# A second buffer for each stage of the pieces of G, in an attention and feed-forward layer on one Trainium2 core

## The reference

```
queries = (query @ Wq + bq); keys_flat = key_param @ Wk + bk
values = keys_flat @ Wv + bv
A = sparsemax(einsum('blhe,bshe->bhls', queries, keys) / sqrt(E))
out = einsum('bhls,bshd->blhd', A, values)   # transposed to (B, H, L, D), then
out = transpose(out, (0, 2, 1, 3)).reshape(B, L, H * D) @ Wo + bo
x = layernorm(x + out)
s = x @ Win + bin_; h = relu(s[..., None] * W1 + b1)
g = einsum('btmh,mh->btm', h, W2) + b2
x = layernorm(x + g @ Wout + bout)
```

## Time and profile before

| | |
|---|---|
| median of three runs | 1370.93 us |
| the profiled execution | 1371.21 us, span 1369.4 us |
| PE busy | 1238.4 us (90%) |
| DVE busy | 1155.0 us (84%) |
| ACT busy | 1078.6 us (79%) |
| POOL busy | 851.5 us (62%) |
| mean granted TensorE clock | 0.952 |
| HBM read, written | 273.24 MB, 58.72 MB |

### The profile page before, as it was taken

How to read it: one execution, slowest core, us unless ns; L and a number is a source line. 1 busy time by engine, 2 the same in 40 slices (tenths; PEclk the granted TensorE clock), 3 DMA queues, 4 the chain that set the end, 5 groups by cost and what they waited for, 6 DMA issues and landing times. The chain is left out here.

```text
span 1369.4 us, 25981 instructions
## 1 busy us (share of the span) xinstructions
PE 1238.4 (90%) x6104; PEld 917.0 (67%) x6104; DVE 1155.0 (84%) x4538; ACT 1078.6 (79%) x2317; POOL 851.5 (62%) x1676
## 2 busy tenths in 40 slices
PE   9954557599999999999999999999999999989885
PEld 6632334477777777777777777777777777756552
DVE  4847555798999999999999999999999999957666
ACT  3634254467899999999999999999999999977666
POOL 1532334454567777777777777777777767766654
PEclk9976667899999999999999999999999999999998
DMA  6455355898778788888888888888888888789983
GB/s 202 124 135 146 76 143 147 235 333 254 247 259 268 266 265 263 270 274 270 266 266 266 261 270 273 276 263 268 266 263 265 271 275 265 241 268 345 333 274 100
DMA packets 96793, 333.89 MB, mean 244 GB/s; under 512 B 16580, under 2 KB 16580, under 8 KB 80231
## 3 DMA queue, kind: packets, MB, share of 16 engines
q1 hardware_dynamic: 96470, 331.76, 76.4%
q10 hardware_dynamic: 144, 0.26, 0.1%
HBM read 273.24 MB, written 58.72 MB: 242 GB/s over the span
## 5 line engine op out<-in xcount | busy, mean ns | idle before, releaser
L825 PE MATMUL bank<-G_sb,pT 128*128 128x512 f32 x512 | 244.5, 600 | 11.1 <-DMA G_sb<-G_of_heads 9.9
L1462 DVE MAX8 top<-bank 128x8 f32<-128x32 f32 x2048 | 211.4, 175 | 0.0
L816 PE MATMUL bank<-A_hi,xT_hi 128*128 128x512 f32 x512 | 205.3, 401 | 0.0
L817 PE MATMUL bank<-A_lo,xT_hi 128*128 128x512 f32 x512 | 205.2, 401 | 0.0
L818 PE MATMUL bank<-A_hi,xT_lo 128*128 128x512 f32 x512 | 204.7, 400 | 0.0
L1512 DVE SCALAR_TENSOR_TENSOR acc<-hinge,w2c,acc 128x512 f32<-128x512 f32 x210 | 156.5, 745 | 51.9 <-ACT hinge L1096 51.7
L605 POOL TENSOR_TENSOR rstd<-ve,minus_half 128x1 f32<-128x1 f32 x244 | 172.9, 709 | 43.0 <-POOL ve L600 42.7
L1066 ACT ACTIVATE unread<-y_sb,minus_mean 128x512 bf16<-128x512 f32 x244 | 174.5, 715 | 24.6 <-POOL minus_mean L592 23.6
L1096 ACT ACTIVATE hinge<-s_sb,b1c,w1c 128x512 f32<-128x512 f32 x240 | 192.6, 805 | 0.0
L592 POOL TENSOR_TENSOR minus_mean<-sum,per_row 128x1 f32<-128x1 f32 x244 | 86.1, 359 | 133.9 <-DVE y_sb L1355 133.6
L1355 DVE SCALAR_TENSOR_TENSOR y_sb<-bank,y_sb 128x512 f32<-128x512 f32 x244 | 159.3, 657 | 10.0 <-DMA y_sb<-in_L_attn_query_dram 8.8
(11 more groups left out here) (172 smaller groups left out, 3144.8 us busy)
## 6 DMA issues: line engine op xcount, KB each, us to landing
G_sb<-G_of_heads SPq DMA_DIRECT2D x128, 1536.0 KB, 7.7
x_sb<-in_L_attn_query_dram SPq DMA_DIRECT2D x128, 256.0 KB, 6.5
y_sb<-in_L_attn_query_dram SPq DMA_DIRECT2D x256, 128.0 KB, 7.2
out_dram<-o_sb SPq DMA_DIRECT2D x230, 128.0 KB, 6.5
G_of_heads<-y_sb SPq DMA_DIRECT2D x96, 256.0 KB, 4.1
out_dram<-y_sb SPq DMA_DIRECT2D x11, 256.0 KB, 3.3
y_sb<-in_L_attn_Wk_dram SPq DMA_DIRECT2D x1, 1024.0 KB, 5.7
y_sb<-in_L_attn_Wq_dram SPq DMA_DIRECT2D x1, 1024.0 KB, 7.9
```

The costliest lines, as they stand in the source:

```text
L816: nc.tensor.matmul(ps[:], hi[:, c, :], w_hi[:, c, :], start=start and c == 0, stop=False)
L817: nc.tensor.matmul(ps[:], hi[:, c, :], w_lo[:, c, :], start=False, stop=False)
L825: nc.tensor.matmul(o[:], p_blocks[:, block_of(i, c), i % HPC, :], G[:, raw_col(c), :].bitcast(F32), start=(c == RAW[0]), stop=False)
L1462: mx = nc.vector.max(top8[:, h, :], z_ps[i % 2][:, h * S:(h + 1) * S])
```

## The change

Each of the three stages gets a second buffer, used in turns by successive units of its kind:

- plain: rows 0 to 3 of `y_sb`, and the four rows of `o_sb` (the ring of the finished rows, not used before slot 36);
- rests: rows 4 to 7 and 8 to 11 of `y_sb`;
- rounded parts: four of the six rows in `G_sb` buffer 1, and in buffer 2.

ScalarE waits, before it fills a buffer, for the stores of the unit before the last one of its kind. SyncE stores plain and rounded parts in its slot u+6 instead of u+7; rests stay in slot u+8. The loads of G for heads 1 and 2, which overwrite the rounded parts' buffers, wait for their stores and for the subtractions that read them. The waits ahead of the y loads follow the new rows. The row of b_out, loaded at the start and read at slot 25, moves from `o_sb` to `both`. ScalarE's and POOL's instructions stay in the order in which they were, with other tiles; the rest is now written as plain float32, without rounding.

```diff
-        STAGE_RAW, STAGE_LO, STAGE_HI = 0, HPC, 2 * HPC
+        def stage_raw(k):
+            return (y_sb[:, 0:HPC, :], o_sb[:])[k // (2 * HPC) % 2]
+        def stage_lo(k):
+            first = HPC * (1 + k // (2 * HPC) % 2)
+            return y_sb[:, first:first + HPC, :]
+        def stage_hi(k):
+            return G_sb[:, 1 + k // (2 * HPC) % 2, 0:HPC, :]
...
@@ SyncE, slot
-                for k in pieces(turn, j - 2)[HPC - 1:]:
+                for k in pieces(turn, j - 1)[HPC - 1:]:
                     heads, c, a = piece(k)
                     if in_parts(k):
                         sp.wait_ge(s_Ghi, parts_to(k))
-                        store_unit(heads, hi_col(c), STAGE_HI, s_Gst_hi)
+                        store_unit(heads, hi_col(c), stage_hi(k).bitcast(F32), s_Gst_hi)
                     else:
                         sp.wait_ge(s_Gev, k + 1)
-                        store_unit(heads, raw_col(c), STAGE_RAW, s_Gst_raw)
+                        store_unit(heads, raw_col(c), stage_raw(k), s_Gst_raw)
                 for k in pieces(turn, j - 3)[HPC - 1:]:
                     heads, c, a = piece(k)
                     if in_parts(k):
                         sp.wait_ge(s_Glo, parts_to(k))
-                        store_unit(heads, lo_col(c), STAGE_LO, s_Gst_lo)
+                        store_unit(heads, lo_col(c), stage_lo(k), s_Gst_lo)
...
+                    if i in (1, 2):
+                        sp.wait_ge(s_Glo, PIECES // 2 - (HPC if i == 1 else 0))
+                        sp.wait_ge(s_Gst_hi, 16 * (PIECES // 2 - (HPC if i == 1 else 0)))
...
-                    for row, s_stored in ((STAGE_RAW, s_Gst_raw), (STAGE_LO, s_Gst_lo), (STAGE_HI, s_Gst_hi)):
-                        if base + i == row:
-                            sp.wait_ge(s_stored, 16 * (PIECES // 2))
+                    if base + i == 0:
+                        sp.wait_ge(s_Gst_raw, 16 * (PIECES // 2))
+                    if base + i == HPC:
+                        sp.wait_ge(s_Gst_lo, 16 * (PIECES // 2))
@@ POOL, slot
-                        nc.gpsimd.tensor_tensor(y_sb[:, STAGE_LO + a, :].bitcast(F32R), y_sb[:, STAGE_LO + a, :],
-                                                y_sb[:, STAGE_HI + a, :], ALU.subtract).then_inc(s_Glo, 1)
+                        lo, hi = stage_lo(k)[:, a, :], stage_hi(k)[:, a, :]
+                        nc.gpsimd.tensor_tensor(lo, lo, hi.bitcast(F32), ALU.subtract).then_inc(s_Glo, 1)
@@ ScalarE, slot
-                    stored = 16 * HPC * (k // HPC // 2)
+                    stored = 16 * HPC * (k // HPC // 2 - 1)
                     if in_parts(k):
-                        if a == 0 and k >= 2 * HPC:
+                        if a == 0 and stored > 0:
                             act.wait_ge(s_Gst_hi, stored)
                             act.wait_ge(s_Gst_lo, stored)
```

More of the change, by code:

```diff
@@ L193, in build_kernel @@
         Wout_sb = s_sb[:, 0, :]
-        bout_row = o_sb[0:1, 2, :]
+        bout_row = both[0:1, :]
         rounded = split[0:1, :]
@@ L487, in store_unit @@
                     sp.dma_start(places[:, :, col * D:(col + 1) * D],
-                                 y_sb[n * S:(n + 1) * S, stage:stage + HPC, :]).then_inc(s_stored, 16)
+                                 stage[n * S:(n + 1) * S]).then_inc(s_stored, 16)
             def slot(turn, j):
@@ L1189, in slot @@
                     act.wait_ge(s_Gmm, k + 1)
-                    stored = 16 * HPC * (k // HPC // 2)
+                    stored = 16 * HPC * (k // HPC // 2 - 1)
                     if in_parts(k):
-                        if a == 0 and k >= 2 * HPC:
+                        if a == 0 and stored > 0:
                             act.wait_ge(s_Gst_hi, stored)
                             act.wait_ge(s_Gst_lo, stored)
-                        nc.scalar.copy(y_sb[:, STAGE_LO + a, :], G_ps[a][:]).then_inc(s_Gev, 1)
-                        nc.scalar.copy(y_sb[:, STAGE_HI + a, :].bitcast(F32R), G_ps[a][:]).then_inc(s_Ghi, 1)
+                        nc.scalar.copy(stage_lo(k)[:, a, :], G_ps[a][:]).then_inc(s_Gev, 1)
+                        nc.scalar.copy(stage_hi(k)[:, a, :], G_ps[a][:]).then_inc(s_Ghi, 1)
                     else:
-                        if a == 0 and k >= 2 * HPC:
+                        if a == 0 and stored > 0:
                             act.wait_ge(s_Gst_raw, stored)
-                        nc.scalar.copy(y_sb[:, STAGE_RAW + a, :], G_ps[a][:]).then_inc(s_Gev, 1)
+                        nc.scalar.copy(stage_raw(k)[:, a, :], G_ps[a][:]).then_inc(s_Gev, 1)
             slots(act, slot)
```

## The result

The changed kernel took 1315.93 us (median of four runs, 1312.34 to 1319.75) against 1370.85 for the kernel before on the same chip: a ratio of 0.960, 95% interval 0.957 to 0.963. The profiled execution is the slowest of the four, 1319.75 us with a span of 1318.0, so it shows 51.4 us of gain where the median shows 54.9.

The account below looks back on a forecast made before the run. TensorE was taken to bound the long middle, which early savings move forward whole: 10.8 + 41.4 + 9.55 = 61.75 us, less 3.0 at the handover, 58.75 off 1371.21: 1312.5, as a median 1312 us; range 1304 to 1319.

Parts of the forecast that it names:

- The wait and its cause: While G is made, ScalarE waits 71.5 us in 7 waits for the previous odd unit's stores, having one buffer.
- u1 to u3: First to second odd (rounded part and rest) unit of G, start to start: 23.82 us now, 13.0 after.
- The four gated pairs: Four odd-unit-to-odd-unit stretches outside the sort, paced by stores after the change: 103.4 us to 62.0, gain 41.4.
- The loop: Odd unit to odd unit through SyncE's queue: 4.04 us copies, then eight stores at 6.4 + 4.5; 14.9, say 15.0.
- the 16.0: Length in us taken for each of the two pairs where the probabilities' transposes join, within 14 to 18.
- The sign of a DMA share near 0.9: If right, the profile after shows DMA engines' busy share near 0.9 in the early part that makes G.
- u5 to u9: Third to fifth odd unit, over VectorE's sort: 67.55 us, of which only the last wait, 9.55, is gained.
- the wait under the sort: ScalarE's 10.59 us wait inside VectorE's sort of a tile; removing it was claimed to be worth nothing.
- The handover: From making G to PE's first products: G loads queued behind stores come late, costing 3.0 us (bounds 0 and 8).
- u15: Last of the eight odd units of G; predicted to start near 186 us after the change.
- Rival A: TensorE's clock stays low: pairs with probabilities 18.15 us, others 17, handover 5; gain 48.5, 1322 us; chance 0.19.
- The rule on ports: Stores reading 32 partitions reach 8 of 16 ports, 218 GB/s at most; by it the run ends near 1318 us.

Follow-up runs that it names:

- the variant with rests first: Against the changed kernel, SyncE's slot stores the ready rest ahead of the plain or rounded part; 1307.59 us, ratio 0.9527 to the kernel before.

## Why the prediction was right, point by point

**The wait and its cause: right.** Two buffers alone take ScalarE's waits for stores from 71.5 us to 0; sooner stores with one buffer leave 70.7. POOL's two subtractions took 2.71 us before and after, so the rests as plain float32 cost nothing, as assumed.

**u1 to u3, gain 10.8: measured 10.9.** 12.90 us start to start.

**The four gated pairs, 62.0 for 103.4: measured 62.6** (15.56, 14.45, 17.93, 14.61). The sum fits better than its parts, and that is in part luck. The loop was put at 4.04 + 6.4 + 4.5 = 14.9 and is 4.04 + 10.47 = 14.5; it sets the two pairs without probabilities, as the variant with rests first shows. In the two others the loop isn't what is last: ScalarE waits for PE, 0.19 us, not for stores. They are set by the engines and by TensorE's clock, 14.8 to 17.9 us over ten profiles, and the 16.0 was right as a mean of values that differ from execution to execution. The sign of a DMA share near 0.9 came only in part: from pair to pair it was 0.68 to 0.92.

**u5 to u9, 67.55 to 58.0: measured 57.67.** That the wait under the sort is free was shown by putting it back. In other profiles this stretch took 57.6 to 59.7 us, so the near hit is partly luck too.

**The handover, 3.0 late: measured 3.16** at the first product and 2.88 at the third, by the cause given for the first: the load moved ahead of the stores takes it away. The sum had 2.5 at the first and 3 at the third, so the first was 0.7 more and nothing was added behind it. It didn't all last, though DMA was to give nothing back: at the ninth product 2.2 of it are left, 59.10 us sooner against 61.28 at u15.

**What was missed.** The sum says 58.75, and at tiles 8 to 104 the trace shows 59.10. The profiled execution ends 51.4 us sooner. The missing term is the end of the run, which the prediction took as moved whole: there the loads of G and TensorE's clock set the pace, and neither is the same in each execution. Of the 7.7 us 4.0 go with slower loads and the rest with the clock. The median of these four runs is 4 us over the 1312 foreseen, within the range; the median of six runs of the same kernel later was 1312.60, so much of the 4 us is spread. Rival A's mechanism (a clock that stays low) is real, but only in part as it was told: of its two pairs with probabilities one took 17.93 us, near the 18.15 it gave, and the other 15.56; the pairs without them kept a clock of 1.00 and took 14.5 us, not 17.

**The rule on ports.** In the changed kernel, between 88 and 92 us, when that block of stores filled the queue, DMA moved 241 GB/s. The 218 GB/s that "SBUF — State Buffer" (the Trainium skill, section "Door 1: The DMA port swizzle") allows a store of 32 partitions is not a bound for such stores in a row, of which the four of a unit read four different quarters of the partitions; it changed nothing in the sum. The page's figure is for one transfer, and no run here has a store by itself.

## What to carry to other kernels

Where a producer waits for a buffer to be stored, count what stands between the last write and the landing: other engines' slots, then the queue. Here a second buffer took all of it off the path. Asking sooner with one buffer took nothing off, and with two it cost some 5 us, because in an in-order queue a ready store stood behind one that waited for something newer. Before pricing waits by their sum, look for one that lies under another stall (10.96 us for at most 1.7, against 10.73 that cost 11 to 13.5), and price the clock that an idle TensorE comes back with. Leave a few us for what is behind the change: an end that waits for loads does not simply move forward.

## What the runs showed of the hardware that was not expected

The stretch in which DMA is full, tiles 116 to 124, moved 318 to 348 GB/s in different executions of nearly the same code, with the share of busy DMA engines at 1.02 or 1.03 in each. Of the same kernel one profile had 348 GB/s and the next 329. These eight tiles took 46.5 to 52.1 us by it, a difference as large as what several of the edits were worth. What decides it stays open.
